# A post-norm transformer block on one core: later batches of x stored whole and split on return, one batch's rows stored after the last maxima

## The chip, the cores and the metric

The kernel runs on one core of a Trainium2 chip. The metric is device time in microseconds of one execution. Engines are TensorE (PE; its weight loads are PEld), VectorE (DVE), ScalarE (ACT), GpSimd (POOL) and SyncE (SP), which here only issues DMAs. ScalarE has a DMA queue of its own as well.

## The reference

The input x has 4 batches of 1024 tokens of 256 features. The block is causal attention with 16 heads of 64 and rotary positions, a layer norm, a mixture of 16 experts of which each token takes 3, and a second layer norm:

```python
x = _layernorm(x + _L0_attn_ref(x, W_in, b_in, W_out, b_out))   # 4 x 1024 x 256, H=16, KD=VD=64
x = _layernorm(x + _L0_ffn_ref(x, gate, W1, b1, W2, b2))        # E=16, top 3, hidden 512
```

All of it is float32. The change touches the attention phase only.

## The kernel before

**Two-part operands.** TensorE's fast format (fp32r) keeps fewer bits than float32. So each operand of the q/k/v projections, x and W_in, is held as a high part (a copy rounded to fp32r, made by ScalarE) and a low part (the operand less its high part, a subtraction on VectorE), and a projection is the sum of high x high, high x low and low x high: `PRODUCTS`, twelve matmuls per projection unit (L583).

**Setup (L270 to L358, L530 to L560, L740 to L760, L845 to L860).** x and the weights are transposed on TensorE (L541) into PSUM banks in units of 512 columns: 12 weight units, 4 units of x per batch, 4 of W_out. For each unit ScalarE writes the high part (`high_halves`, L751) and VectorE the low part (`low_halves`, L856). The weight parts go to the table `wsplit` in DRAM (12 stores of 512 KB, L308). Batch 0 stays in the tile `xT` (index 0 high, 1 low). The units of batches 1 to 3 are transposed after the second projection of pair 0 (`late_transposes`), by ScalarE after the fourth rope copy of pair 0 (`finish_high_halves`), and both their parts are stored in the table `xsplit` (L323, 12 stores of 512 KB); until then they lie in tiles that attention does not need yet (`x_place`). The last two projections of pair 0 come behind them.

**Turns.** Attention takes 32 steps, `n` = batch x 8 + pair of heads. The loop `turns` runs `it` from -2 to 32, and each engine goes through a fixed list per turn: `PE_ORDER`, `ACT_ORDER`, `DVE_ORDER`, `POOL_ORDER`, `SP_ORDER`. A + or - after an event says that it is for a later or earlier step, so `F0++` in turn `it` is of step `it + 2`. The events that matter here:
- F0 to F3: the projections of a step into `g_ps` (F0, F1: q and k for tokens 0 to 511 and 512 to 1023; F2, F3: v). r0 to r3 on VectorE multiply q and k by the rotary tables (L929), a and l on GpSimd add the halves and make the low part (L499, L504), h on ScalarE makes the high part (L803).
- W and S on SP: the high and low parts of q and k go to the table `hilo` (`put_halves`, L336) and come back stacked (`stack`, L350 and L347), in halves c = 0 and 1.
- A: scores by query (L591) whose row maxima VectorE takes (M; L909, L913). One bank per head, so A of one block waits for M of the block before. X transposes the maxima (L700); w on ScalarE (L794) copies them and issues the DMA that puts them as a row beside q (L797).
- B: scores by key less the row of maxima (L598, L599), E: their exponentials on ScalarE (L790). k0 to k3 and K are sums of them on VectorE (L952) and GpSimd (L526), V the product with v (L680), D, R, G and O the normalization and output projection.
- L on SP: loads of the next weights (L406, L410) and, in every eighth turn, the next batch's x from `xsplit` into `xT` (`load_x`, L358, 1 MB for each half of the tokens: half 0 after F0, half 1 after F3 of the batch's last step).
- y and `move_tile`: the first layer norm of a finished batch, spread over the next batch's turns. In the turns 14, 22 and 30 SP stores the rows of batch 0, 1 and 2, two stores of 128 KB per tile, to `xn` and `sum0` (L379, L380).

F0 and F1 of a batch's first step wait for the two halves of x; they are in turns 6, 14 and 22, called borders here. B0 and B4 wait for the rows of maxima of the two halves.

Behind attention come routing, the experts and the final sum with the second layer norm; the change leaves them alone.

Of the kernel before, what the change touches and what calls it, by code (L numbers as in the profile page):

```python
# [17 lines left out]
P = 128  # L18
# [22 lines left out]
ACT_ORDER = parse("""E0.0 E0.1 E1.0 E1.1 E2.0 w1 E2.1 E3.0 d1- h0++ N1- E3.1 E4.0 E4.1 y0 h1++ E5.0 d0 h2++ E5.1 E6.0 N0 E6.1 y1 E7.0  # L41
w0+ E8.0 E7.1 h3++ E8.1 y2 E9.0 E9.1 y3 E10.0 v2++ E10.1 E11.0 E11.1 v3++""")
DVE_ORDER = parse("""M11.1 M0.0+ C0 M0.1+ M1.0+ M1.1+ M2.0+ k0 M2.1+ M3.0+ k1 k2 r0++ M3.1+ R4- r1++ R5- M4.1+ k3 M4.0+ R6- R7-
# [90 lines left out]
def attention_phase(nc, A, dram, shared):  # L134
    x, W_in, b_in, W_out, cosT, sinT = A["x"], A["W_in"], A["b_in"], A["W_out"], A["cos"], A["sin"]
    xsplit, wsplit = dram["xsplit"], dram["wsplit"]
    hilo = dram["hilo"]
    vo = shared["vo"]
    with ExitStack() as ctx:
# [52 lines left out]
        xsp = [sem(f"xsp{b}") for b in range(B)]  # L192
# [40 lines left out]
        for what, p in W_UNITS:  # L233
# [3 lines left out]
        v_flat = v_sb[:, 1].rearrange("p t s c -> p (t s c)").bitcast(F32R)  # L237
        prob_r = prob[:].bitcast(F32R)

        x_place = [[[xT[:, a, k, :] for k in range(DK)] for a in range(2)],  # L240
                   [[q2_flat[1][:, k, :] for k in range(DK)], [v_flat[:, k * T:(k + 1) * T] for k in range(DK)]],
                   [[prob_r[:, (2 * a + k) * T:(2 * a + k + 1) * T] for k in range(DK)] for a in range(2)],
                   [[t[1][:, k, :] for k in range(DK)] for t in (q1, k1)]]

        def setup_places(u):

            if u < NW:
                return w_place[u][:, 0], w_place[u][:, 1]
            b, k, c = X_UNITS[u - NW]
            return [x_place[b][a][k][:, 512 * c:512 * c + 512] for a in range(2)]  # L250
# [20 lines left out]
        def _(sp):  # L271
# [33 lines left out]
            for i, (what, p) in enumerate(W_UNITS):  # L305
                sp.wait_ge(m["setup_hi"], i + 1)
                sp.wait_ge(m["setup_lo"], i + 1)
                sp.dma_start(wsplit[p if what == "qk" else PAIRS + p].rearrange("p (a k c) -> p a k c", a=2, k=DK),  # L308
                             w_place[i].bitcast(F32)).then_inc(m["wsp"], 16)

            sp.wait_ge(m["setup_hi"], EARLY)
# [5 lines left out]
            def put_x(b):  # L317
                sp.wait_ge(m["setup_hi"], NW + 4 * (b + 1))
                sp.wait_ge(m["setup_lo"], NW + 4 * (b + 1))
                dst = xsplit[b].rearrange("p (a k c) -> p a k c", a=2, k=DK)  # L320
                for a in range(2):
                    for k in range(DK):
                        sp.dma_start(dst[:, a, k], x_place[b][a][k].bitcast(F32)).then_inc(xsp[b], 16)  # L323
# [33 lines left out]
            def load_x(batch, c):  # L357
                sp.dma_start(xT[:, :, :, 512 * c:512 * c + 512].bitcast(F32),  # L358
                             row(xsplit, batch).rearrange("p (a k c) -> p a k c", a=2, k=DK)
                             [:, :, :, 512 * c:512 * c + 512]).then_inc(x_ld[c], 16)  # L360
# [11 lines left out]

            def move_tile(b, place, i):
# [3 lines left out]
                if place == LN_STORE and b < B - 1:  # L377
                    sp.wait_ge(m["normed"], TB * b + i + 1)
                    sp.dma_start(xn[b][:, i, :], rows).then_inc(m["x_st"], 16)  # L379
                    sp.dma_start(first_sum[:, TB * b + i, :], rows).then_inc(m["x_st"], 16)  # L380
# [4 lines left out]
            def turn(it, place):  # L385

                for i, (e, ahead) in enumerate(SP_ORDER):
# [8 lines left out]
                    elif kind == "S":  # L396
                        if n == 1 and c == 0:
                            for b in range(1, B):
                                sp.wait_ge(xsp[b], 64)
                        stack(n, s, c // 2, c % 2)  # L400
                    elif c == 0:
                        if more:
                            sp.wait_ge(m["p_fill"], 4 * n + 1)
                            load_x((n + 1) // PAIRS, 0)
                        sp.wait_ge(m["p_fill"], 4 * n + 2)
                        sp.dma_start(flat(w_sb[s]), row(wsplit, (place + ahead + 2) % PAIRS)).then_inc(w_ld[s], 16)  # L406
                    else:
# [4 lines left out]
                        if more:  # L412
                            load_x((n + 1) // PAIRS, 1)
# [1419 lines left out]
```

## Time and profile before

| | us |
|---|---|
| median of 3 runs (1835.59 to 1837.06) | 1836.42 |
| profiled execution, its own time | 1841.24 |
| its span | 1839.4 |
| TensorE busy | 1691.7 (92%) |
| VectorE busy | 1380.8 (75%) |
| GpSimd busy | 1234.6 (67%) |
| ScalarE busy | 729.2 (40%) |
| mean granted clock of TensorE | 0.958 |

The span runs from the first to the last instruction. Matmuls are pipelined, so TensorE's busy share is not its share of peak. The granted clock is a share of 2.4 GHz. "Idle before" in a row is the time for which the engine had no instruction running, with what released it; a letter q behind an engine means its queue, which issues DMAs. Attention ends near 1290 us.

### The profile page before, as it was taken

What the parts mean: (1) busy time and instruction counts of PE and PEld (TensorE: products, weight loads), DVE (VectorE), ACT (ScalarE), POOL (GpSimd) and SP (SyncE); (2) the same over time, 40 slices, a digit from 0 to 9 for tenths busy, and PEclk for the clock granted to TensorE, in tenths of its full rate; (3) what the DMA queues carried; (4) which work ended last, traced back from release to release, by engine and by line L of the source; (5) the groups of instructions that cost most, each with busy time, mean ns of one, the idle gap of its engine ahead of it and who ended that gap; (6) DMA issues with size and microseconds to landing.
All of it is one profiled execution on the core that took longest, in us unless ns stands there. A gap on an engine that the chain in (4) does not pass through costs nothing. (4 is left out here: it accounts for less than half of the span.)

```text
span 1839.4 us, 34097 instructions
## 1 busy us (share of the span) xinstructions
PE 1691.7 (92%) x9515; PEld 1265.7 (69%) x9516; DVE 1380.8 (75%) x3236; ACT 729.2 (40%) x1551; POOL 1234.6 (67%) x1064
## 2 busy tenths in 40 slices
PE   4689999999999999999999999998649999999990
PEld 4566667666766677667766676654339999999980
DVE  3578888888888888888888888865775656656654
ACT  2234444444445544444444444543352222222222
POOL 2256788677877776788777777755017777777764
PEclk8699999999999999999999999989859999999995
DMA  9976556655655776556676664550964444444448
GB/s 308 335 204 163 157 166 202 178 171 151 183 161 173 230 219 190 157 166 198 210 215 187 179 177 138 161 152 1 339 186 70 72 72 75 71 72 74 71 65 277
DMA packets 185572, 302.39 MB, mean 164 GB/s; under 512 B 23632, under 2 KB 82896, under 8 KB 185312
## 3 DMA queue, kind: packets, MB, share of 16 engines
q1 hardware_dynamic: 161872, 269.20, 49.2%
q0 software_dynamic: 21504, 30.29, 10.2%
q10 hardware_dynamic: 2064, 1.31, 0.3%
q8 instruction: 61, 1.00, 0.2%
q14 instruction: 71, 0.58, 0.1%
HBM read 188.81 MB, written 111.67 MB: 163 GB/s over the span
## 5 line engine op out<-in xcount | busy, mean ns | idle before, releaser
L790 ACT ACTIVATE prob<-b_ps 128x512 f32<-128x512 f32 (+3 forms) x768 | 354.5, 488 | 366.7 <-PE b_ps L599 263.8
L526 POOL TENSOR_TENSOR acc<-acc,prob 128x1024 f32<-128x1024 f32 (+1 forms) x192 | 353.0, 1838 | 6.4 <-ACT prob L790 3.3
L598 PE MATMUL b_ps<-q,k 128*128 128x512 f32 (+3 forms) x768 | 296.9, 391 | 7.6 <-ACT prob L790 3.7
L499 POOL TENSOR_TENSOR roped<-rot 128x512 f32<-128x512 f32 x128 | 174.8, 1366 | 166.8 <-DVE rot L929 166.0
L591 PE MATMUL a_ps<-k,q 128*128 128x512 f32 (+3 forms) x768 | 266.7, 384 | 18.2 <-DMA k<-scratch_hilo 8.2
L680 PE MATMUL y_ps<-prob,v_sb 128*64 128x512 f32 (+3 forms) x1536 | 274.9, 493 | 0.1
L909 DVE CUSTOM_DVE_ANT_0 masked<-a_ps,causal 128x128 bf16<-128x128 f32 (+3 forms) x512 | 237.4, 479 | 48.4 <-PE a_ps L591 40.5
L599 PE MATMUL b_ps<-q,k 65*128 65x512 f32 (+3 forms) x768 | 265.0, 349 | 0.0
L1479 POOL DMA_INDIRECT scratch_sum<-y,dst_i x112 | 186.9, 1669 | 94.7 <-ACT y L1551 89.8
L958 DVE RECIPROCAL inv<-inv 128x128 f32<-128x128 f32 x256 | 232.3, 930 | 7.7 <-ACT inv L831 5.3
L504 POOL TENSOR_TENSOR lo<-roped,hi 128x512 fp32r<-128x512 f32 x128 | 177.8, 1389 | 81.1 <-ACT hi L803 81.1
L680 PEld LDWEIGHTS y_ps<-prob,v_sb 128*64 128x64 f32 x1536 | 104.7, 137 | 180.9 <-issue 176.1
L1505 PEld LDWEIGHTS h_ps<-mxT,w_now 128*128 128x128 f32 x1792 | 218.7, 193 | 5.7
L1505 PE MATMUL h_ps<-mxT,w_now 128*128 128x128 f32 x1792 | 219.1, 276 | 0.0
L1514 PE MATMUL yo_ps<-w,hT 128*128 x896 | 211.8, 379 | 0.0
L913 DVE TENSOR_REDUCE max_b<-a_ps 128x1 f32<-128x512 f32 x256 | 171.9, 672 | 41.2 <-PE a_ps L591 37.9
L583 PE MATMUL g_ps<-xT,w_sb 128*128 128x512 f32 x768 | 195.4, 405 | 7.4 <-DVE rot L929 4.5
L598 PEld LDWEIGHTS b_ps<-q,k 128*128 128x128 f32 x768 | 145.3, 189 | 77.2 <-issue 44.9
L591 PEld LDWEIGHTS a_ps<-k,q 128*128 128x128 f32 x768 | 143.2, 192 | 63.3 <-DVE max_b L913 12.3
L1464 POOL DMA_INDIRECT xin<-scratch_xn,src_i x112 | 111.7, 997 | 108.2 <-POOLq L999 74.4
L583 PEld LDWEIGHTS g_ps<-xT,w_sb 128*128 128x128 f32 x768 | 148.7, 197 | 40.3 <-DVE rot L929 5.5
L1514 PEld LDWEIGHTS yo_ps<-w,hT 128*128 128x128 f32 x896 | 161.6, 190 | 17.4
(258 smaller groups left out, 2389.7 us busy)
## 6 DMA issues: line engine op xcount, KB each, us to landing
q<-scratch_hilo SPq DMA_DIRECT2D x192, 256.0 KB, 4.6
k<-scratch_hilo SPq DMA_DIRECT2D x192, 256.0 KB, 5.2
scratch_hilo<-hi SPq DMA_DIRECT2D x64, 512.0 KB, 4.1
scratch_hilo<-lo SPq DMA_DIRECT2D x64, 512.0 KB, 4.7
w_sb<-scratch_wsplit SPq DMA_DIRECT2D x32, 512.0 KB, 3.5
w<-in_L_ffn_W_dram SPq DMA_DIRECT2D x32, 512.0 KB, 10.0
wv_sb<-scratch_wsplit SPq DMA_DIRECT2D x16, 512.0 KB, 7.2
xT<-scratch_xsplit SPq DMA_DIRECT2D x6, 1024.0 KB, 6.6
```

What stands on the lines that cost most here:

```text
L526: nc.gpsimd.tensor_tensor(sums, old, probs(q), ALU.add).then_inc(m["sum_p"], 1)
L583: ins = nc.tensor.matmul(out, left, right, start=(a, b, k) == PRODUCTS[0], stop=(a, b, k) == PRODUCTS[-1], skip_group_check=True)
L591: nc.tensor.matmul(out, q1[s][:, h, blk * P:(blk + 1) * P], k1[s][:, h, k0:k0 + w], start=True, stop=True, skip_group_check=True).then_inc ...
L598: nc.tensor.matmul(out, k1[s][:, h, js], q1[s][:, h, qs], start=True, stop=False, skip_group_check=True)
L599: ins = nc.tensor.matmul(out, k2[s][0:65, h, js], q2[s][0:65, half, h, 512 - w:512], start=False, stop=True, skip_group_check=True)
L680: ins = nc.tensor.matmul(y_ps[64 * h:64 * h + 64, 512 - w:512], v_sb[:, pairs, j, s, 64 * h:64 * h + 64], probs(q)[:, h, :], start=(j == 0 ...
L790: nc.scalar.activation(probs(q)[:, h, :], b_ps[:, h, 0:w], ACT.Exp).then_inc(exp_done[h], 1)
L909: nc.vector.tensor_tensor_reduce(masked[:, h, 0:w], a_ps[:, h, 0:w], causal[:, 512 - w:512], -1.0, -MASKED, ALU.add, ALU.min, out).then_in ...
L958: nc.vector.reciprocal(part, part).then_inc(inv_done[c], 1)
L1479: pool.indirect_dma_start(out=dram[f"sum{t % SUMS}"], out_offset=bass.IndirectOffsetOnAxis(ap=dst_i[:, t:t + 1], axis=0), in_=y[:, t % 2, ...
L1505: ins = nc.tensor.matmul(h_ps[:, s, c * P:(c + 1) * P], w1_now[:, s, k, c * P:(c + 1) * P], xT[:, s, k * P:(k + 1) * P], start=(k == 0), s ...
L1514: ins = nc.tensor.matmul(yo_ps[:, s, 0:D], hT[:, s, c * P:(c + 1) * P], w2[:, bass.ds(e, 1), c, :].rearrange("p a d -> p (a d)"), start=(c ...
```

## The change

What it does, part by part:
- Batches 1 to 3 of x are not split in setup. ScalarE copies each transposed unit as float32 into one whole tile per batch (`x_whole`), and a batch is one store of 1 MB to the table `xturned`, half the bytes of `xsplit`; the 12 subtractions of these batches and TensorE's waits for them are gone.
- On return a half of 512 tokens (512 KB instead of 1 MB) goes to the low place of `xT`. Half 0 is issued by SP as before; half 1 by ScalarE's queue, right behind the last v copy of the batch's last step. New events `s0++` and `s1++` split it: ScalarE copies to the high place (two copies per half), VectorE subtracts in place (two per half). F0 and F1 wait for the subtractions.
- SP stores the six weight units that lie in the way of pair 0's stacks first (`WAITED`), then pair 0's first halves, three other weights, the first stack, the other three weights, the second halves and stack, and then x.
- The rows of batch 2 are stored after the turns, once the last row of maxima has landed (`m_ld`), and no longer in turn 30.

The diff, cut to its core:

```diff
-ACT_ORDER = parse("""E0.0 E0.1 E1.0 E1.1 E2.0 w1 E2.1 E3.0 d1- h0++ N1- E3.1 E4.0 E4.1 y0 h1++ E5.0 d0 h2++ E5.1 E6.0 N0 E6.1 y1 E7.0
+ACT_ORDER = parse("""E0.0 E0.1 s0++ E1.0 E1.1 E2.0 w1 E2.1 s1++ E3.0 d1- h0++ N1- E3.1 E4.0 E4.1 y0 h1++ E5.0 d0 h2++ E5.1 E6.0 N0 E6.1 y1 E7.0
 w0+ E8.0 E7.1 h3++ E8.1 y2 E9.0 E9.1 y3 E10.0 v2++ E10.1 E11.0 E11.1 v3++""")
-DVE_ORDER = parse("""M11.1 M0.0+ C0 M0.1+ M1.0+ M1.1+ M2.0+ k0 M2.1+ M3.0+ k1 k2 r0++ M3.1+ R4- r1++ R5- M4.1+ k3 M4.0+ R6- R7-
+DVE_ORDER = parse("""M11.1 M0.0+ C0 M0.1+ s0++ M1.0+ M1.1+ M2.0+ k0 M2.1+ M3.0+ k1 k2 r0++ M3.1+ s1++ R4- r1++ R5- M4.1+ k3 M4.0+ R6- R7-
 M5.0+ r2++ G1- r3++ z0 M5.1+ o1- M6.0+ R0 M6.1+ R1 M7.0+ R2 R3 G0 z1 M7.1+ o2- M8.0+ M8.1+ M9.0+ o3- M9.1+ M10.0+
...
-        v_flat = v_sb[:, 1].rearrange("p t s c -> p (t s c)").bitcast(F32R)
-        prob_r = prob[:].bitcast(F32R)
-
-        x_place = [[[xT[:, a, k, :] for k in range(DK)] for a in range(2)],
-                   [[q2_flat[1][:, k, :] for k in range(DK)], [v_flat[:, k * T:(k + 1) * T] for k in range(DK)]],
-                   [[prob_r[:, (2 * a + k) * T:(2 * a + k + 1) * T] for k in range(DK)] for a in range(2)],
-                   [[t[1][:, k, :] for k in range(DK)] for t in (q1, k1)]]
+        v_flat = v_sb[:, 1].rearrange("p t s c -> p (t s c)")
+        x_whole = [None] + [t.rearrange("p (k c) -> p k c", k=DK)
+                            for t in (v_flat[:, 0:DK * T], prob[:, 0:DK * T], prob[:, DK * T:2 * DK * T])]
         def setup_places(u):
             if u < NW:
                 return w_place[u][:, 0], w_place[u][:, 1]
             b, k, c = X_UNITS[u - NW]
-            return [x_place[b][a][k][:, 512 * c:512 * c + 512] for a in range(2)]
+            cs = slice(512 * c, 512 * c + 512)
+            return [xT[:, a, k, cs] for a in range(2)] if b == 0 else [x_whole[b][:, k, cs]]
+        WAITED = [u for u in range(NW) if W_UNITS[u][0] == "qk" and 2 <= W_UNITS[u][1]]
+        OTHERS = [u for u in range(NW) if u not in WAITED]
+        def splits_before(n, c):
+            return 4 * (n // PAIRS - 1) + 2 * c
...
+            def put_weights(units, stored):
+                for i in units:
+                    what, p = W_UNITS[i]
+                    sp.wait_ge(m["setup_hi"], i + 1)
+                    sp.wait_ge(m["setup_lo"], i + 1)
+                    sp.dma_start(wsplit[p if what == "qk" else PAIRS + p].rearrange("p (a k c) -> p a k c", a=2, k=DK),
+                                 w_place[i].bitcast(F32)).then_inc(stored, 16)
+            put_weights(WAITED, wsp_first)
...
             def put_x(b):
                 sp.wait_ge(m["setup_hi"], NW + 4 * (b + 1))
-                sp.wait_ge(m["setup_lo"], NW + 4 * (b + 1))
-                dst = xsplit[b].rearrange("p (a k c) -> p a k c", a=2, k=DK)
-                for a in range(2):
-                    for k in range(DK):
-                        sp.dma_start(dst[:, a, k], x_place[b][a][k].bitcast(F32)).then_inc(xsp[b], 16)
+                sp.dma_start(xturned[b].rearrange("p (k c) -> p k c", k=DK), x_whole[b]).then_inc(xsp[b], 16)
...
-            def load_x(batch, c):
-                sp.dma_start(xT[:, :, :, 512 * c:512 * c + 512].bitcast(F32),
-                             row(xsplit, batch).rearrange("p (a k c) -> p a k c", a=2, k=DK)
-                             [:, :, :, 512 * c:512 * c + 512]).then_inc(x_ld[c], 16)
+            def load_x(batch):
+                sp.dma_start(xT[:, 1, :, 0:512].bitcast(F32),
+                             row(xturned, batch).rearrange("p (k c) -> p k c", k=DK)[:, :, 0:512]).then_inc(x_ld[0], 16)
...
+            def put_tile(b, i):
+                rows = x1[:, b % 2 * TB + i, :]
+                sp.wait_ge(m["normed"], TB * b + i + 1)
+                sp.dma_start(xn[b][:, i, :], rows).then_inc(m["x_st"], 16)
+                sp.dma_start(first_sum[:, TB * b + i, :], rows).then_inc(m["x_st"], 16)
             def move_tile(b, place, i):
                 rows = x1[:, b % 2 * TB + i, :]
-                if place == LN_STORE and b < B - 1:
-                    sp.wait_ge(m["normed"], TB * b + i + 1)
-                    sp.dma_start(xn[b][:, i, :], rows).then_inc(m["x_st"], 16)
-                    sp.dma_start(first_sum[:, TB * b + i, :], rows).then_inc(m["x_st"], 16)
+                if place == LN_STORE and b < B - 2:
+                    put_tile(b, i)
...
-                        if n == 1 and c == 0:
-                            for b in range(1, B):
-                                sp.wait_ge(xsp[b], 64)
...
-            for c in range(2):
-                put_halves(0, 0, c)
-            sp.wait_ge(m["wsp"], 16 * NW)
-            for c in range(2):
-                for second in range(2):
-                    stack(0, 0, c, second)
-                put_x(1 + c)
-            put_x(3)
+            put_halves(0, 0, 0)
+            put_weights(OTHERS[:3], m["wsp"])
+            sp.wait_ge(wsp_first, 16 * len(WAITED))
+            for second in range(2):
+                stack(0, 0, 0, second)
+            put_weights(OTHERS[3:], m["wsp"])
+            put_halves(0, 0, 1)
+            for second in range(2):
+                stack(0, 0, 1, second)
+            for b in (2, 3, 1):
+                put_x(b)
+            sp.wait_ge(m["wsp"], 16 * len(OTHERS))
             for it in range(-2, STEPS):
                 turn(it, it)
+            for c in range(2):
+                sp.wait_ge(m_ld[c], 16 * STEPS)
+            for i in range(TB):
+                put_tile(B - 2, i)
...
-                    pe.wait_ge(m["setup_lo"], old + 1)
+                    if u < EARLY:
+                        pe.wait_ge(m["setup_lo"], old + 1)
...
-                        if q < 2 and not first:
-                            pe.wait_ge(x_ld[q], 16 * (n // PAIRS + 1))
+                        if q < 2 and n >= PAIRS:
+                            pe.wait_ge(m["setup_lo"], EARLY + splits_before(n, q) + 2)
...
+                    elif kind == "s":
+                        if n % PAIRS or n == 0:
+                            continue
+                        act.wait_ge(x_ld[q], 16 * (n // PAIRS + 1))
+                        for k in range(DK):
+                            nc.scalar.activation(xT[:, 0, k, 512 * q:512 * q + 512],
+                                                 xT[:, 1, k, 512 * q:512 * q + 512].bitcast(F32),
+                                                 ACT.Copy).then_inc(m["setup_hi"], 1)
...
+                        if q == 3 and n % PAIRS == PAIRS - 1 and n + 1 < STEPS:
+                            act.dma_start(xT[:, 1, :, 512:T].bitcast(F32),
+                                          xturned[(n + 1) // PAIRS].rearrange("p (k c) -> p k c", k=DK)[:, :, 512:T])\
+                                .then_inc(x_ld[1], 16)
...
+                    elif kind == "s":
+                        if n % PAIRS or n == 0:
+                            continue
+                        for k in range(DK):
+                            dve.wait_ge(m["setup_hi"], NW + NX + splits_before(n, q) + k + 1)
+                            low = xT[:, 1, k, 512 * q:512 * q + 512]
+                            nc.vector.tensor_tensor(low, low.bitcast(F32), xT[:, 0, k, 512 * q:512 * q + 512].bitcast(F32),
+                                                    ALU.subtract).then_inc(m["setup_lo"], 1)
...
-                        if n == 0 and q == 3:
-                            low_halves(EARLY, NW + NX)
```

Three places show what moved. SP's queue in the opening, before, from the last rows of the weight stores: `wsplit` is the weights' table, `hilo` the table of q and k, whose halves come back into the q and k tiles, `xsplit` the table of split x.

```order
L308 DMA scratch_wsplit<-q_1 128x1024 x2
L308 DMA scratch_wsplit<-k_1 128x1024
L336 DMA scratch_hilo<-hi 256x1x512
L336 DMA scratch_hilo<-lo 256x1x512
L336 DMA scratch_hilo<-hi 256x1x512
L336 DMA scratch_hilo<-lo 256x1x512
L350 DMA q_0<-scratch_hilo 64x2x512 x2
L350 DMA k_0<-scratch_hilo 64x2x512 x2
L347 DMA q_0<-scratch_hilo 64x2x512
L347 DMA k_0<-scratch_hilo 64x2x512
L323 DMA scratch_xsplit<-q_1 128x1024 x2
```

And of the change, from the first weight stores:

```order
L316 DMA scratch_wsplit<-q_0 128x1024 x2
L316 DMA scratch_wsplit<-k_0 128x1024 x2
L316 DMA scratch_wsplit<-q_0 128x1024 x2
L341 DMA scratch_hilo<-hi 256x1x512
L341 DMA scratch_hilo<-lo 256x1x512
L316 DMA scratch_wsplit<-w_sb 128x1024 x2
L316 DMA scratch_wsplit<-wv_sb 128x1024
L355 DMA q_0<-scratch_hilo 64x2x512 x2
L355 DMA k_0<-scratch_hilo 64x2x512 x2
L352 DMA q_0<-scratch_hilo 64x2x512
L352 DMA k_0<-scratch_hilo 64x2x512
L316 DMA scratch_wsplit<-q_1 128x1024 x2
```

Six weight stores, not twelve, stand before the first hi and lo of pair 0; the second hi and lo moved behind the first stack and three more weight stores; x has three stores, and they come after the second stack.

VectorE at the start of turn 6, before, from the maxima of the first block of scores (128x128) to those of the second (128x256):

```order
L909 ISA masked,max_a<-a_ps,causal 128x128
L909 ISA max_a 128x1
L920 TENSOR_TENSOR max_c<-max_b 128x8
L909 ISA masked,max_a<-a_ps,causal 128x128
L909 ISA max_a 128x1
L909 ISA masked,max_a<-a_ps,causal 128x256
L909 ISA max_a 128x1
L909 ISA masked,max_a<-a_ps,causal 128x256
```

And of the change:

```order
L931 ISA masked,max_a<-a_ps,causal 128x128
L931 ISA max_a 128x1
L950 TENSOR_TENSOR max_c<-max_b 128x8
L931 ISA masked,max_a<-a_ps,causal 128x128
L931 ISA max_a 128x1
L945 TENSOR_TENSOR xT<-xT 128x512 x2
L931 ISA masked,max_a<-a_ps,causal 128x256
L931 ISA max_a 128x1
```

The two subtractions of x's first half stand before the maxima of the second block (128x256). The other two stand behind the fourth block's second maxima, before the second rope:

```order
L959 SCALAR_TENSOR_TENSOR rot<-g_ps,bias,cos_sb 128x512
L959 SCALAR_TENSOR_TENSOR rot<-g_ps,bias,sin_sb 128x512
L931 ISA masked,max_a<-a_ps,causal 128x512
L931 ISA max_a 128x1
L945 TENSOR_TENSOR xT<-xT 128x512 x2
L986 RECIPROCAL inv<-inv 128x128
L959 SCALAR_TENSOR_TENSOR rot<-g_ps,bias,cos_sb 128x512
L959 SCALAR_TENSOR_TENSOR rot<-g_ps,bias,sin_sb 128x512
L986 RECIPROCAL inv<-inv 128x128
```

ScalarE's copies for them stand behind the first two exponentials of the turn and behind the sixth.

## Rows read from the trace of the kernel before

**Rows 1.** Windows: length, busy us (PE, PEld, DVE, ACT, POOL), clock, DMA share, GB/s
```profile
34.00:40.00 6.00, 4.98 (x13) 3.87 (x14) 0.96 (x2) 0.74 (x2) 3.83 (x3) 0.54 1.03 418
...
110.00:116.00 6.00, 5.67 (x18) 4.55 (x19) 2.27 (x5) 1.21 (x2) 3.60 (x4) 0.72 0.39 80
...
200.00:300.00 100.00, 100.00 (x535) 71.26 (x535) 86.36 (x187) 45.13 (x97) 77.46 (x68) 1.00 0.61 171
```

**Rows 2.** The query by line, transposes of the first maxima: duration, first and last start
```profile
L700 PE MATMUL t_ps<-ident,max_a x32: 271/273/274, 81.8 to 1234.8; 128*8 128x128 f32 x32
```

**Rows 3.** TensorE's waits: total us, times, longest
```profile
PE a_ps L591 <- DMA k<-scratch_hilo: 8.2, 4, 3.5
```

**Rows 4.** The timeline, opening: start, us, engine, line; copies and transposes
```profile
46.96 1.07 ACT L751 ACTIVATE q<-b_ps 128x512 fp32r<-128x512 f32 x2
...
48.41 1.09 PE L541 MATMUL b_ps<-ident,yT 128*128 128x128 f32 x4 [6.57 <-DVE v_sb L856]
...
56.28 1.19 ACT L757 ACTIVATE woT<-a_ps 128x512 f32<-128x512 f32 x2
```

**Rows 5.** The timeline, opening: a load of the table, TensorE after it
```profile
54.71 1.28 SPq L350 DMA_DIRECT2D q<-scratch_hilo  x2
...
62.62 0.44 PE L591 MATMUL a_ps<-k,q 128*128 128x128 f32 x2 [1.95 <-DMA k<-scratch_hilo]
...
74.80 1.22 PE L591 MATMUL a_ps<-k,q 128*128 128x512 f32 x2 [3.48 <-DMA k<-scratch_hilo]
...
75.88 5.12 PE L583 MATMUL g_ps<-xT,w_sb 128*128 128x512 f32 x12
```

**Rows 6.** The timeline, turn 0: VectorE's rope and TensorE
```profile
109.40 0.74 DVE L929 SCALAR_TENSOR_TENSOR rot<-g_ps,bias,sin_sb 128x512 f32<-128x512 f32 x1
...
110.33 0.73 PE L591 MATMUL a_ps<-k,q 128*128 128x512 f32 x2 [2.35 <-DMA k<-scratch_hilo]
...
111.53 4.34 PE L583 MATMUL g_ps<-xT,w_sb 128*128 128x512 f32 x12
```

**Rows 7.** The timeline, start of turn 6: exponentials, maxima, TensorE
```profile
320.70 1.79 ACT L790 ACTIVATE prob<-b_ps 128x512 f32<-128x512 f32 x3
...
321.63 0.42 DVE L909 CUSTOM_DVE_ANT_0 masked<-a_ps,causal 128x256 bf16<-128x256 f32 x1
...
322.11 0.19 PEld L591 LDWEIGHTS a_ps<-k,q 128*128 128x128 f32 x1 [0.16 <-DVE max_a L909]
```

**Rows 8.** The timeline, turn 6: GpSimd's add, the second rope, its projection
```profile
328.28 1.27 POOL L499 TENSOR_TENSOR roped<-rot 128x512 f32<-128x512 f32 x1 [2.48 <-DVE rot L929]
...
330.33 0.74 DVE L929 SCALAR_TENSOR_TENSOR rot<-g_ps,bias,sin_sb 128x512 f32<-128x512 f32 x1
...
332.33 2.90 PE L583 MATMUL g_ps<-xT,w_sb 128*128 128x512 f32 x12
```

**Rows 9.** The timeline, VectorE with two inputs: setup, turn 6, turn 31
```profile
16.50 0.69 DVE L856 TENSOR_TENSOR q<-a_ps,q 128x512 fp32r<-128x512 f32 x1 [0.16 <-ACT q L751]
...
332.67 0.88 DVE L952 TENSOR_TENSOR acc<-acc,prob 128x256 f32<-128x256 f32 x1
...
1257.24 0.42 DVE L952 TENSOR_TENSOR acc<-acc,prob 128x256 f32<-128x256 f32 x1 [0.83 <-ACT prob L790]
```

**Rows 10.** The timeline, turns 30 and 31: row of maxima, TensorE
```profile
1214.28 0.63 ACTq L797 DMA_DIRECT2D q<-mrow  x1
...
1220.99 0.77 PE L598 MATMUL b_ps<-q,k 128*128 128x512 f32 x1 [2.47 <-DMA q<-mrow]
...
1231.55 0.50 PE L598 MATMUL b_ps<-q,k 128*128 128x512 f32 x1
...
1255.87 0.45 PE L598 MATMUL b_ps<-q,k 128*128 128x512 f32 x1
...
1261.07 0.50 PE L598 MATMUL b_ps<-q,k 128*128 128x512 f32 x1
```

**Rows 11.** The windows, turn 30
```profile
1221.00:1224.00 3.00, 2.89 (x6) 1.78 (x6) 0.92 (x2) 0.67 (x2) 0.00 (x0) 0.50 0.81 274
```

More of the change, by code:

```diff
@@ L135, in attention_phase @@
     x, W_in, b_in, W_out, cosT, sinT = A["x"], A["W_in"], A["b_in"], A["W_out"], A["cos"], A["sin"]
-    xsplit, wsplit = dram["xsplit"], dram["wsplit"]
+    xturned, wsplit = dram["xturned"], dram["wsplit"]
     hilo = dram["hilo"]
@@ L191, in attention_phase @@
         m = {k: sem(k) for k in names}
-        xsp = [sem(f"xsp{b}") for b in range(B)]
+        wsp_first = sem("wsp_first")
+        xsp = [None] + [sem(f"xsp{b}") for b in range(1, B)]
         x_in = [sem(f"x_in{b}") for b in range(B)]
@@ L303, in _ @@
             sp.dma_start(wo_raw, W_out.rearrange("(r p) c -> p r c", p=P)).then_inc(m["wo_in"], 16)
[L305 to L309, printed above, removed]
+            def put_weights(units, stored):
[6 more added lines that the diff above has]
+            put_weights(WAITED, wsp_first)
             sp.wait_ge(m["setup_hi"], EARLY)
@@ L403, in turn @@
                             sp.wait_ge(m["p_fill"], 4 * n + 1)
-                            load_x((n + 1) // PAIRS, 0)
+                            load_x((n + 1) // PAIRS)
                         sp.wait_ge(m["p_fill"], 4 * n + 2)
@@ L411, in turn @@
                                 .then_inc(m["wv_ld"], 16)
-                        if more:
-                            load_x((n + 1) // PAIRS, 1)
                 if ZEROS_FROM <= it < ZEROS_FROM + ZERO_PIECES:
@@ L554, in late_transposes @@
                     transposes(NW + NX + i, [wo_raw[:, r, (4 * c + j) * P:(4 * c + j + 1) * P] for j in range(4)])
-                pe.wait_ge(m["setup_lo"], NW + NX)
                 pe.wait_ge(m["wo_ev"], len(WO_UNITS))
@@ L744, in high_halves @@
                     act.wait_ge(m["setup_tr"], u + 1)
-                    if u >= NW and X_UNITS[u - NW] == (3, 0, 0):
-                        act.wait_ge(m["wsp"], 16 * NW)
                     src = setup_bank(u)
@@ L772, in turn @@
                             for b in range(1, B):
-                                act.wait_ge(xsp[b], 64)
+                                act.wait_ge(xsp[b], 16)
                         act.wait_ge(b_fill[h], UNITS * n + q + 1)
@@ L1789, in scratch @@
 def scratch(nc):
-    shapes = {"xsplit": [B, P, 2 * DK * T], "wsplit": [PAIRS + PAIRS // 2, P, 2 * DK * 256], "hilo": [2, 2, P, 2, T], "xn": [NTOK, E_ + D]}
+    shapes = {"xturned": [B, P, DK * T], "wsplit": [PAIRS + PAIRS // 2, P, 2 * DK * 256], "hilo": [2, 2, P, 2, T], "xn": [NTOK, E_ + D]}
     shapes.update({f"sum{i}": [NTOK + P, D] for i in range(SUMS)})
```

## The prediction

> **What bounds the kernel now.** I read the windows first. In the middle of attention TensorE is busy for all 100 us of 100, at a granted clock of 1.00, its 2.4 GHz [rows 1]; a turn lasts 37.2 us on average, 31 of them from 81.8 to 1234.8 us [rows 2]. So in a turn nothing is gained by taking work off another engine, and each us for which TensorE is made to wait is a us of the end. The list of its waits and the timeline say where it does wait: 6.57 us once for a low half of x, at 48.41; 8.2 us in four waits for k from the hi/lo table [rows 3], the three large ones at 62.62, 74.80 and 110.33; and 2.47 us for the row of maxima at 1220.99, in turn 30 [rows 4, 5, 6, 10]. The change can win only there. It can lose wherever a new wait enters a full turn.
>
> **The opening.** Batches 1 to 3 are no longer split: 12 subtractions leave VectorE, and 3 MB of 6 leave the stores. The copies of those units begin at 46.96; ScalarE is held until then by the rope of pair 0, so the wait of 6.57 us hardly shrinks. The last of 16 copies ends at 57.47, after steps partly in turn with VectorE. ScalarE alone does two in 1.07 us, so twelve in 6.4, and the four of W_out at 0.60 in 2.4: the end comes at 55.8, 1.6 us sooner [rows 4]. The last two projections of pair 0 then end at 59.1 instead of 60.7 (62.62 less 1.95), where the first score waits for k [rows 5]. That load was issued at 54.71, behind twelve weight stores and the first hi/lo halves. A store of 512 KB takes 1.25 us at the 418 GB/s of a full queue [rows 1]. Six fewer stand ahead now, so it is issued at about 47.2. From issue to use it took 7.9 us; with the three weight stores that stand before it added (3.8) it is there at 58.9, and the wait goes. Scores start 3.5 us sooner.
>
> The second half of pair 0 gains less. Its path is 47.2, three stores (3.8), six loads (1.5 MB; 7.5 us if a load of 256 KB takes as long as a store, half that at the full rate), three stores and two halves (6.3), and 7.9 from issue to use: 72.7 or 68.9, against 74.80 now, so 2.1 us, or at most 3.5, since the rope would then set the projection that follows at 75.88. I take 2.4, between them and nearer to the slow one, as loads of 2 KB rows are; 1.0 is kept as the low end. Pair 1's first half then comes in time (0.4, the smallest of the four waits). The 2.35 us at 110.33 go as well, since 3 MB of stores, 7.5 us, no longer lie in the queue; but the projection behind them needs VectorE's rope, which ends at 110.14, so it moves only from 111.53 to 110.2: 1.3 us. It ran in 4.34 us, where twelve such matmuls take 2.90 at full clock [rows 6, 8], because the clock fell behind that idle stretch: 0.72 over these 6 us [rows 1]. With 1.1 us idle instead of 2.35 I expect it full: 1.4 us more (bounds 0 and 1.4). Opening: 2.4 + 0.4 + 1.3 + 1.4 = **5.5 us gained** (2.7 to 6.6).
>
> **Turn 30.** The row of maxima is issued at 1214.28; TensorE is ready at 1218.5 and waits until 1220.99 [rows 10]; then the clock reads 0.50, 1.2 GHz [rows 11]. Sixteen stores of batch 2's rows share the DMA engines there. They now go out after the last row of maxima, under work of turn 31. What stays ahead is 1 MB of loads, 2.5 us at the full rate, which would end before 1218.5 and leave no wait; the other end is no gain at all. I take 1.6 of the 2.47, nearer to the first. With 0.9 us idle the clock should hold. From this matmul to the one at 1231.55 it is 10.56 us; in turn 31 the same work but for three score matmuls takes 5.20 (1255.87 to 1261.07), and those three with a wait for VectorE make some 2.1: 3.3 us saved. Together **4.9 us** (bounds 0 and 5.8). The stores' new place costs nothing: SP's queue holds nothing else then, and 16 stores of 128 KB are 5 us at the full rate, under a turn.
>
> **The borders, turns 6, 14 and 22.** Each gains four copies on ScalarE and four subtractions on VectorE. Start of the turn: ScalarE's second exponential ends near 321.9 (three in 1.79 us from 320.70). Then come a copy of 128x512 (0.60, an exponential's) and a subtraction (0.69, the setup's, [rows 9]); the second copy is hidden, the second subtraction is not. The next maxima began at 321.63; now at 321.9 + 0.6 + 0.69 + 0.69 = 323.9. TensorE already waits 0.16 us for just these [rows 7], and its stream is in order, so it stands still for **2.25 us** in front of the first projection. Behind that projection the other two subtractions stand before the second rope. This rope ends at 331.07, the projection that needs it starts at 332.33: 1.26 us of slack [rows 8]. Two subtractions are 1.4 us by the plain price. But a VectorE operation with two inputs in SBUF took 0.88 us while GpSimd was adding, and the same shape 0.42 while it was not [rows 9], and an add of GpSimd of 1.27 us falls on this place [rows 8]. So I take 2.1, and 0.9 is left over on TensorE. The Trainium skill has the rule (SBUF — State Buffer, "SBUF: two separate sides"): VectorE with two SBUF inputs and GpSimd shut each other out for a whole instruction. The trace agrees with it; without the rule the leftover would be 0.1. A border costs 3.2 us (2.3 to 4.4, if the backlog also delays the third rope). The issue on ScalarE's queue runs beside a copy of 0.60 us and is taken as free (0.6 at most). Of the smaller loads I count nothing: no wait is theirs today.
>
> On top comes the clock. It fell after 2.35 us of idle time in turn 0 and after 2.47 in turn 30, so a border's 2.25 is on the edge. A fall costs 4.34 - 2.90 = 1.4 us; I count it at one or two borders of three, 2.1 us. Borders: 3 x 3.2 + 2.1 = **11.7 us lost** (7 to 17).
>
> **Sum.** -5.5 - 4.9 + 11.7 = +1.3 us. The profiled execution took 1841.24 us (span 1839.4), 4.8 above the median of the runs shown, 1836.42; applied to the median: **1837.7 us**. Routing, experts and the final sum do not move.
>
> **The rivals.** First, *the splits hide*. For it: VectorE idles 14 us in 100 [rows 1]. Against it: the start of the turn is its densest place. If a border costs 1.5 us and the gains stand, -10.4 + 4.5 = -6: 1830.5. Second, *the clock falls at every border* and VectorE's backlog reaches the third rope: 3 x (4.4 + 1.4) = 17.4, less 10.4: +7, 1843.4. This is the case on the other side; it decides from about 2.3 us of idle time at a border, and a copy 0.1 us slower than I take it is enough. The Trainium skill (TensorE: Matmul & The Clock Gate, "HAM oscillation — how this bites in real kernels") warns of idle gaps that put TensorE back to half its clock; the rows of turns 0 and 30 agree. Third, *the stores were not the cause*: the row of maxima lands late behind the 1 MB of loads alone, and x's second half, on ScalarE's queue but the same engines, holds ScalarE: +1.3 + 4.9 = +6, 1842.6. By the Trainium skill (DMA: Bandwidth & Descriptors, "Issuing engines are not separate DMA queues") a second queue saves only the issue; no run here shows that. That the change does not do what it says has no room: the printed order shows each moved row.
>
> **How the numbers follow.** The sum as worked out, 0.42; splits hide, 0.27; clock at every border, 0.18; stores not the cause, 0.13. A measurement of this kernel tells 0.2%, 3.7 us, from no change. So faster 0.27, same 0.42, slower 0.31. The likeliest case alone has 1834 to 1840. The range goes from 1829.5 (opening and end at their upper bounds, -12.4, borders at 1.8 each, +5.4) to 1845 (the second rival with 4 us of opening: 17.4 - 8.9 = +8.5).
>
> **What would show it.** Right: the waits at 62.62 and 1220.99 gone or under 1 us, clock 1.00 through turn 30, and in turns 6, 14 and 22 a wait of some 2 us of TensorE for the maxima behind the first split. Wrong: border turns that last no longer than before, or a clock of 0.50 in each of them, or the row of maxima still awaited for over 2 us in turn 30.

## The result and the profile after

The changed kernel takes 1843.82 us (median of 19 runs) and the kernel before 1837.11 us (19 runs): a ratio of 1.0034, with a 95% interval of 1.0026 to 1.0042. So it is slower by 0.34%, 6.3 us, above the 1837.7 us forecast and inside the range of 1829.5 to 1845.0. The prediction drew its own line between same and slower at 3.7 us; by that line this is slower. The profiled execution took 1846.57 us (span 1844.4).

TensorE's waits in the list by line, in the columns of [rows 3]:

```profile
PE a_ps L604 <- DVE max_a L931: 6.7, 6, 2.0
PE g_ps L596 <- DVE rot L959: 6.5, 4, 4.5
...
PE a_ps L604 <- DMA k<-scratch_hilo: 5.5, 1, 5.5
PE b_ps L611 <- DMA q<-mrow: 5.4, 3, 2.8
```

Four waits for k (8.2 us) have become one of 5.5. New are three waits of 2 us for the maxima (first line), three of 0.67 for the rope (in the second, beside an old one of 4.5), and three for a row of maxima, where the kernel before had 2.7 us in two. To see what this does to a turn, take the transposes of the first maxima, [rows 2], in pairs: first and last start of two neighbours are one turn apart. After, for turns 0, 6, 14, 22 and 30:

```profile
L713 PE MATMUL t_ps<-ident,max_a x2: 272/272/273, 78.0 to 119.8; 128*8 128x128 f32 x2
L713 PE MATMUL t_ps<-ident,max_a x2: 273/273/273, 302.5 to 343.6; 128*8 128x128 f32 x2
L713 PE MATMUL t_ps<-ident,max_a x2: 272/272/273, 604.2 to 644.4; 128*8 128x128 f32 x2
L713 PE MATMUL t_ps<-ident,max_a x2: 272/272/273, 903.5 to 945.3; 128*8 128x128 f32 x2
L713 PE MATMUL t_ps<-ident,max_a x2: 273/274/274, 1205.8 to 1239.5; 128*8 128x128 f32 x2
```

And before, turns 0 and 30:

```profile
L700 PE MATMUL t_ps<-ident,max_a x2: 271/272/274, 81.8 to 122.2; 128*8 128x128 f32 x2
L700 PE MATMUL t_ps<-ident,max_a x2: 273/274/274, 1194.7 to 1234.8; 128*8 128x128 f32 x2
```

The opening gave 3.8 us up to the first transpose, of which turn 0 took 1.4 back. The borders last 41.2, 40.2 and 41.7 us instead of 37.0, 37.4 and 37.5: 11.2 us lost. Turn 30 fell from 40.1 to 33.7: 6.4 gained. From the last transpose to the end both need 604.7 to 604.9 us. The other turns add some 2.4 us, which closes the account to the 5.0 us between the spans; nearly all of it are waits of 1.21 and 1.32 us for a row of maxima in turns 10 and 23.

A border in the timeline, turn 6, beside [rows 7, 8]:

```profile
319.19 1.14 ACT L814 ACTIVATE xT<-xT 128x512 fp32r<-128x512 f32 x2
...
319.85 1.29 DVE L945 TENSOR_TENSOR xT<-xT 128x512 fp32r<-128x512 f32 x2 [0.74 <-ACT xT L814]
321.06 0.41 DVE L931 CUSTOM_DVE_ANT_0 masked<-a_ps,causal 128x256 bf16<-128x256 f32 x1
...
321.54 0.44 PE L604 MATMUL a_ps<-k,q 128*128 128x384 f32 x1 [1.99 <-DVE max_a L931]
...
323.65 4.03 PE L596 MATMUL g_ps<-xT,w_sb 128*128 128x512 f32 x12
327.16 1.15 ACT L814 ACTIVATE xT<-xT 128x512 fp32r<-128x512 f32 x2 [2.76 <-DMA xT<-scratch_xturned]
...
329.21 1.27 POOL L512 TENSOR_TENSOR roped<-rot 128x512 f32<-128x512 f32 x1 [3.90 <-DVE rot L959]
...
329.65 1.99 DVE L945 TENSOR_TENSOR xT<-xT 128x512 fp32r<-128x512 f32 x2
...
333.78 0.50 PE L596 MATMUL g_ps<-xT,w_sb 128*128 128x512 f32 x1 [0.67 <-DVE rot L959]
```

VectorE sits idle for 0.74 us until the copy is there, subtracts for 1.29, and only then takes the maxima for which TensorE has been waiting 1.99 us. The projection behind it takes 4.03 us instead of 2.90, for the clock has fallen. Two subtractions of the second half take 1.99 us beside GpSimd's add, and 0.67 is left over for TensorE. The windows of turns 6, 22, 14 and 30, in the columns of [rows 1]:

```profile
323.00:325.00 2.00, 2.00 (x7) 1.68 (x7) 1.99 (x5) 0.65 (x3) 0.85 (x2) 0.50 1.08 255
924.00:926.00 2.00, 2.00 (x9) 1.81 (x8) 1.17 (x6) 1.02 (x3) 0.41 (x1) 0.50 1.02 369
625.00:627.00 2.00, 2.00 (x11) 1.67 (x11) 1.89 (x6) 1.27 (x5) 0.58 (x2) 1.00 1.02 363
1213.00:1223.00 10.00, 10.00 (x62) 8.52 (x60) 7.74 (x19) 4.93 (x12) 9.83 (x9) 1.00 0.85 246
```

The clock is 0.50 behind the wait of turns 6 and 22 and 1.00 behind that of turn 14, and it stays at 1.00 through turn 30.

In turn 0 the wait for k at 110.33 [rows 6] is gone, and one for the row of maxima is there (run 2 will show that the old opening can have that one too). The timeline, TensorE in the opening, then ScalarE's queue and TensorE in turn 0:

```profile
71.09 1.22 PE L604 MATMUL a_ps<-k,q 128*128 128x512 f32 x2 [5.46 <-DMA k<-scratch_hilo]
...
100.48 0.63 ACTq L807 DMA_DIRECT2D q<-mrow  x1
...
107.61 0.77 PE L611 MATMUL b_ps<-q,k 128*128 128x512 f32 x1 [2.83 <-DMA q<-mrow]
```

The wait in turn 10 has no store of rows near it. SP's load of 512 KB ahead of it, the row's own DMA, and TensorE:

```profile
468.73 0.33 SPq L417 DMA_DIRECT2D wv_sb<-scratch_wsplit  x1
...
472.62 0.63 ACTq L807 DMA_DIRECT2D q<-mrow  x1
...
480.68 0.47 PE L611 MATMUL b_ps<-q,k 128*128 128x512 f32 x1 [1.21 <-DMA q<-mrow]
```

Between the load of wv_sb and the row stand two loads of 256 KB from the table. Nothing else is issued in the 3.8 us ahead of the row, and yet TensorE gets it only 8.1 us after its issue.

### The profile page after: what moved, and what is told of

Same layout as the page of the kernel before. It is cut to its first block and busy times, and to the rows that moved or that the text cites. A ratio compares the mean times of both kernels' runs of the same rounds, so it can differ in the third digit from the quotient of the medians.

```text
span 1844.4 us, 34087 instructions
## 1 busy us (share of the span) xinstructions
PE 1692.1 (92%) x9515; PEld 1269.9 (69%) x9516; DVE 1379.5 (75%) x3236; ACT 733.9 (40%) x1563; POOL 1234.5 (67%) x1064
## 5 line engine op out<-in xcount | busy, mean ns | idle before, releaser
L525 POOL TENSOR_SCALAR_AFFINE_SELECT prob<-prob 128x256 f32<-128x256 f32 x256 | 110.3, 436 | 95.7 <-ACT prob L800 90.8
```

## The experiments

Theory T after this comparison: the splits cost some 3.7 us a border, and where they stand is the cause; the stores of turn 30 held up the row of maxima; the opening gains, and a new wait in turn 0 limits it. Ratios are to the kernel before, on the same chip; 1 us is 0.00054. Beside the time, the length of single turns is compared, since a run's profile is one execution.

**1. Batch 2's rows in turn 30 again** (the changed kernel otherwise).

```diff
-                if place == LN_STORE and b < B - 2:
+                if place == LN_STORE and b < B - 1:
...
-            for i in range(TB):
-                put_tile(B - 2, i)
```

> The changed kernel, but batch 2's rows are stored in turn 30 again, as before. Theory T (the stores held up the row of maxima; the border turns and not the end cost time): turn 30 lasts some 6.4 us longer than in the changed kernel (40.1 instead of 33.7 us from one transpose of maxima to the next), TensorE waits 2 to 2.5 us for the row of maxima and the clock falls to 0.50 behind it; the whole is 6 us slower than the changed kernel, some 12 us (0.7%) slower than the kernel before. Rival R1 (turn 30's gain comes from the smaller loads of x or from another alignment, not from the stores): turn 30 stays near 34 us and the time within 2 us of the changed kernel.

Measured: 1.0045 (1.003 to 1.0059). Turn 30 lasts 37.6 us, and TensorE waits 0.89 us for the row where the kernel before showed 2.47:

```profile
1226.06 0.47 PE L607 MATMUL b_ps<-q,k 128*128 128x512 f32 x1 [0.89 <-DMA q<-mrow]
```

Against the changed kernel's 1.0034 the stores cost 2 us, with both intervals taken together anything from none to 5 us, and not the 6 of theory T. The two traces with the stores in this place show that the row is late by a different amount in each execution.

**2. The kernel before, with the rows stored last.**

> The kernel before with one part of the change: batch 2's rows are stored after the last row of maxima. Theory T: turn 30 goes from 40.1 to some 33.7 us, all other turns stay, and the whole is 5 to 6.4 us faster than the kernel before (ratio 0.997). Rival R1: turn 30 keeps a wait of 2 us, since the 1 MB of loads alone delay the row of maxima, and the time stays within 1.5 us. Rival R4 (the stores behind the turns delay the start of routing): turn 30 gains and the phase behind it gives 2 us or more back.

Measured: 0.9986 (0.9971 to 1.0), 2.6 us faster (0 to 5.3). Turn 30 lasts 33.7 us and holds no wait for the row, as T had it, but the time gains less than half of 6.4. Routing's first transpose comes 1.0 us later behind the last turn; its last one comes 0.7 us earlier, so of R4 nothing is left in this trace.

Its turn 0, whose opening is that of the kernel before, shows something else. The wait for k at 110.33 isn't there, and TensorE waits for the row of maxima instead:

```profile
111.73 0.77 PE L605 MATMUL b_ps<-q,k 128*128 128x512 f32 x1 [2.87 <-DMA q<-mrow]
```

So neither wait belongs to one kernel. Which of the two comes in turn 0 differs from execution to execution, with the old opening too.

**3. The first half split one turn earlier**, in gaps of VectorE; the second half as before. In this and the next kernels s0 to s3 are VectorE's four subtractions, ScalarE's s0 and s1 the copies of a half.

```diff
-ACT:  E0.0 E0.1 s0++ E1.0        ...  h3++ E8.1
+ACT:  E0.0 E0.1 E1.0             ...  h3++ s0+++ E8.1
-DVE:  M0.1+ s0++ M1.0+   M3.1+ s1++ R4-        M7.1+ o2- M8.0+ M8.1+
+DVE:  M0.1+ M1.0+        M3.1+ s2++ s3++ R4-   M7.1+ s0+++ o2- M8.0+ s1+++ M8.1+
```

> The changed kernel, but the first half of x is copied and subtracted one turn earlier (its load has landed some 10 us before that turn ends), each subtraction in a gap of VectorE. Theory T (a border costs 2.0 us for the first split, 1.2 us for the clock behind it and 0.7 us for the second split): the wait of 2.0 us in front of the border's first projection and the fall of the clock go, turns 6, 14 and 22 last 37.5 to 38.5 us instead of 41.2, 40.2 and 41.7, and the whole is 8 to 10 us faster than the changed kernel, 2 to 4 us faster than the kernel before. Rival R2 (the load of the second half on ScalarE's queue and its split are what costs): the borders keep more than 2 us each. Rival R3 (VectorE is short in that turn anyway, so the work only moves): the turns before the borders grow by 1 us or more each and the gain is under 6 us.

Measured: 0.9977 (0.9963 to 0.9991), 4.2 us faster than the kernel before and some 10.5 faster than the changed one. The waits of 2 us and the falls of the clock are gone; the borders last 38.3 us each, the turns before them 36.7, 37.3 and 37.3 as ever. Theory T holds, R2 and R3 fall. What is left is a wait of 0.59 to 0.68 us for the second rope. The load has landed long before: it is issued at 282.92 and lands at 287.08, and the subtractions run at 304.38 and 306.68. The second of them in the timeline, with GpSimd's add beside it:

```profile
304.85 2.85 POOL L539 TENSOR_TENSOR acc<-acc,prob 128x1024 f32<-128x1024 f32 x1
...
306.68 1.58 DVE L945 TENSOR_TENSOR xT<-xT 128x512 fp32r<-128x512 f32 x1
```

**4. The kernel before with the rows last and the opening's stores sorted** as in the change; x split in setup. (In code: the order of the stores as in the diff ahead, with the weights in q1 and k1 ahead of the other three.)

> The kernel before with batch 2's rows stored last (as in the run beside it) and the weight stores of the opening sorted as in the change, while x is still split in setup and stored as 6 MB. Theory T: most of the opening's gain (scores start sooner) comes from the order of the stores, so this is 1 to 3 us faster than the run with the rows alone, some 8 us faster than the kernel before, and faster than any kernel with splits in the borders as they stand. Rival R5 (the gain comes from the 3 MB fewer): it is within 1 us of the run with the rows alone, or slower, since the later stores collide with the loads of turn 0.

Measured: 1.0005 (0.9991 to 1.0019). Not faster than run 2, rather 3.5 us slower. The first transpose comes at 78.4 (before 81.8), so the order does gain 3.4 us; but 3 MB more stand in the queue, and turn 0 then lasts 44.1 us:

```profile
100.91 0.48 PE L608 MATMUL a_ps<-k,q 128*128 128x128 f32 x1 [5.24 <-DMA k<-scratch_hilo]
```

This is what R5 had: without the halved bytes the order gives back in turn 0 what it gained ahead of it. The intervals of runs 2 and 4 overlap, so the times alone don't prove that it is slower than run 2; that the order alone does not bring the 1 to 3 us of theory T is fairly sure.

**5. The changed kernel again**, beside runs 6 to 8.

> The changed kernel itself, unaltered, beside the three variants on one chip, so that they can be compared with it directly. Theory T: the three borders last 3 to 5.5 us more than the kernel before's each, in any execution; turn 0 has a wait for a row of maxima of 1 to 3 us; whole: ratio 1.0034 as in the first comparison, bounds 1.002 and 1.005.

Measured: 1.0037 (1.0022 to 1.0052). Borders of 41.3, 41.7 and 41.7 us; waits of 2.00, 1.87 and 1.87 us with the clock at 0.50 behind all three; the row of maxima of turn 0 awaited for 1.29 us.

**6. As 3, and in border turns a reciprocal behind the second rope.**

```diff
-DVE, turns 6, 14, 22:  s2++ s3++ R4- r1++
+DVE, turns 6, 14, 22:  s2++ s3++ r1++ R4-
```

> The kernel with the first half split early, and in the three border turns a reciprocal (R4) moved behind the second rope of VectorE, so that the two subtractions of the second half stand where the reciprocal stood. Theory T (what is left at a border is VectorE's backlog of 0.6 us in front of the second projection): this wait goes, and each border gives 0.6 to 1.0 us, 2 to 3 us in all against the kernel with the early split (its ratio was 0.9977), so 0.996 to 0.997. Rival R6 (the backlog only moves on to the third rope or to the output projection that waits for the reciprocal): the borders stay at 38.3 us and the time within 1 us.

Measured: 0.9986 (0.997 to 1.0001). The waits for the second rope are gone and the borders last 38.0 us, 0.3 less than in run 3, which is half of what I expected at the least. In the time nothing shows: run to run its times lie between 1831.3 and 1844.0 us. Neither side was right: the waits went, as T had it, and the time stayed, as R6 had it.

**7. As 6, with turn 0's loads held** until the second row of maxima has landed.

```diff
+                        if it == 0:
+                            sp.wait_ge(m_ld[1], 16)
                         sp.wait_ge(m["p_fill"], 4 * n + 4)
```

> As the run before, and in turn 0 alone SP issues the load of wv_sb (512 KB) and the next two loads of the table hilo only when the second row of maxima has landed. Theory M (these loads stand in front of the 4 KB row of maxima on the DMA engines, and so TensorE waits 0.9 to 2.9 us for it near 105 us): the wait goes, turn 0 lasts 38 us instead of 40 to 42, the whole is 2 to 3 us faster than without. Rival M2 (the row needs its 6 to 7 us whatever is in flight): the wait stays above 1 us and nothing is gained; or the held loads come late and turn 1 waits for k.

Measured: 0.9979 (0.9966 to 0.9992), 1.3 us faster than run 6; the intervals overlap. Turn 0 lasts 38.8 us, and a wait of 0.52 us for the row is left. This proves nothing for M: run 6's own trace has no wait for the row in turn 0 (it lasts 39.9 us there), and the time can't tell the two runs apart.

**8. The loads held in every turn** (`if it >= 0: sp.wait_ge(m_ld[1], 16 * n)` in the same place), and **9. the same kernel once more**, beside runs 10 to 12.

> As the run with turn 0's loads held, but in every turn the load of wv_sb and the two loads behind it wait until the second row of maxima has landed. Theory M: the scattered waits of 0.5 to 1.3 us for rows of maxima in turns 10, 23 and 30 go as well; 0 to 2 us faster than with turn 0 alone. Rival M3 (the held loads are needed at once in later turns, where SP's list is tight): waits for k or for the stack appear in many turns, and the time is 2 us or more worse.

> The fastest kernel so far (first half split early, reciprocal behind the rope, loads held in all turns), unaltered, as the measure for the three beside it: ratio 0.996, its times within some 5 us of each other.

Measured: 0.9959 (0.9948 to 0.9971) and 0.9967 (0.9958 to 0.9976), 7.5 and 6.1 us faster than the kernel before. Run 8 is 3.7 us faster than run 7, with intervals that overlap a little, and some 5 us faster than run 6. In the turns behind turn 0 no wait over 0.1 us for a row of maxima is left, and none for k, so M3 falls. All five traces with the loads held in every turn (runs 8 to 12) are free of waits for the row there, where six of the nine others have one or two of 0.4 to 2.5 us. In turn 0 a wait of 0.54 and 0.30 us stays. The times of twelve executions each lie within 5.4 and 6.2 us, where those of runs 6 and 7 lay within 12.7 and 10.5. So the held loads took some of the spread away; that it was this wait is likely and not shown. This version beats both kernels.

**10. The kernel before with rows last and loads held.**

> The kernel before with two parts: batch 2's rows last, and the loads held in all turns until the second row of maxima has landed; x is split in setup and stored as 6 MB as before. Theory W (x whole is worth it once its splits are early: the opening gains 5 to 6 us at the first transpose of turn 1, the borders lose 2.5 to 3.5): 2 to 4 us slower than the run beside it, ratio near 0.998, with waits for k at 62, 75 and 110 us as in the kernel before. Rival W2 (the hold and the place of the rows made all of the gain): the same as the run beside it or faster.

Measured: 1.0067 (1.005 to 1.0083), 12.3 us slower than before and 18 slower than run 9. W had the sign, not the size, and the reason is one that I had not seen: in the kernel before, SP issues x's second half (1 MB) behind the load that is held now. It goes out at 325.46 instead of 321.06, and at 922.74 in turn 22:

```profile
922.74 0.59 SPq L358 DMA_DIRECT2D xT<-scratch_xsplit  x1
...
933.77 2.47 PE L592 MATMUL g_ps<-xT,w_sb 128*128 128x512 f32 x5 [4.87 <-DMA xT<-scratch_xsplit]
```

So this run doesn't price the whole x by itself. It shows that the hold costs more than it brings while x's half stands behind the held load in SP's list. Whether the other queue or the halved bytes is what spares the changed kernel this, no run separates. Its turn 0 has no wait for k either, against what W had expected at 110 us.

**11. As 9, with the rows in turn 30.**

> The run beside it with batch 2's rows stored in turn 30 again. The two traces with this placing showed waits for the row of maxima of 2.47 and 0.89 us. Theory S (the stores delay it by a different amount in each execution, 0.9 to 2.5 us, and the clock falls only behind the long ones): 2 to 4 us slower on the average, and the times spread wider. As the prediction had it: 4.9 us slower. Rival S2 (with the loads held nothing else stands in front of the row): within 1 us.

Measured: 0.9966 (0.9955 to 0.9977), the same as run 9, as S2 had it. SP's last issue ahead of the row, the row's DMA, and SP's first issues once it has landed:

```profile
1204.96 0.43 SPq L387 DMA_DIRECT2D scratch_sum<-x1b  x1
...
1208.57 0.63 ACTq L809 DMA_DIRECT2D q<-mrow  x1
...
1210.34 0.32 SPq L423 DMA_DIRECT2D wv_sb<-scratch_wsplit  x1
1210.71 0.43 SPq L386 DMA_DIRECT2D scratch_xn<-x1b  x1
```

The hold keeps back more than the load: the stores of seven of the eight tiles stand behind it in SP's list, and they go out at 1210.71 and later. So the run shows that these stores cost nothing when they follow the row. It doesn't show that they were harmless where they stood. Here the row is there at most 1.8 us after its issue. In the kernel before it was issued at 1214.28 and awaited until 1220.99 [rows 10], 6.7 us. In the 3 us ahead of it SP had issued the load of wv_sb, two loads of the table and three stores there, and more stores followed; in run 11 SP had issued nothing for 3.6 us. Which share is the loads' and which the stores', these runs don't separate. Turn 10 of the change has such a wait with loads alone ahead of it.

**12. As 9, with the second halves ahead of the last three weight stores.**

```diff
-            put_weights(OTHERS[3:], m["wsp"])
             put_halves(0, 0, 1)
             for second in range(2):
                 stack(0, 0, 1, second)
+            put_weights(OTHERS[3:], m["wsp"])
```

> The run beside it, but SP issues the last three weight stores of the opening behind pair 0's second halves and their stack instead of ahead of them. TensorE waits 4.7 to 6.9 us for k at 70 to 71 us there. Theory Q (three stores of 512 KB stand in front: 3.8 us at the full rate): this wait shrinks by 3 to 4 us and the whole by as much, ratio 0.994. Rival Q2 (the path is the halves' own: the rope copies they wait for end late, so they cannot be issued sooner, and the table's way out and back takes some 17 us): under 1.5 us. Rival Q3 (the stores then collide with turn 0's loads, and the row of maxima or k is late there): gained at 70, given back near 90 to 110.

Measured: 0.9959 (0.9944 to 0.9974), not told apart from run 9.

```profile
66.49 1.05 PE L610 MATMUL a_ps<-k,q 128*128 128x512 f32 x2 [1.39 <-DMA k<-scratch_hilo]
...
69.24 2.31 PE L602 MATMUL g_ps<-xT,w_sb 128*128 128x512 f32 x5 [1.70 <-DVE rot L965]
...
103.48 1.12 PE L610 MATMUL a_ps<-k,q 128*128 128x512 f32 x2 [1.69 <-DMA k<-scratch_hilo]
```

The wait for k shrinks from 6.9 to 1.4 us, as Q had it, but the rope is late next (1.7), and a wait for k appears in turn 0 (1.7): the first transpose comes 2.3 us sooner than in run 9, the second 1.4. That is Q with Q3's return; the time can't tell it.

## Why the prediction was right in its range and wrong in its number

**The opening: forecast 5.5, found 6.1, by other steps.** That the totals are close is luck. Over the five traces with the changed opening as it stands (the change, runs 1, 3, 5, 6) the first transpose comes at 76.8 us on average and the second at 116.9; over the two with the old one (before, run 2) at 81.9 and 123.1. Ahead of turn 0 the gain is thus 5.1, where I had 2.4. The wait at 62.62 went as said, but I took the second half at 72.7, "nearer to the slow one", and it is used at 70.0 to 71.1, in the middle of my two ends. That is 4.1 us sooner on average, more than the "at most 3.5": I had kept the rope where it was, and it ends at 69.7 instead of 75.8. Most of the last us is the clock's: the projection behind it took 5.12 us before and 3.8 to 5.1 after. In turn 0 the gain is 1.1 instead of 3.1 (0.4 + 1.3 + 1.4). The step that failed is "The 2.35 us at 110.33 go as well": that was one execution. Of the three traces with the old opening (before, runs 2 and 10) only the first has this wait, and run 2 has 2.87 us for the row of maxima in its place. With the new opening TensorE waits 0.9 to 2.8 us for the row in four of the five traces, with a fall of the clock behind all but the shortest wait.

**Borders: forecast 11.7, found 12.2.** The three traces with these borders (the change, runs 1 and 5) give 11.2, 12.5 and 12.8 us over the kernel before. The mechanism was right in each part: the first split keeps TensorE waiting for 1.86 to 2.00 us (I had 2.25), the second for 0.67 (I had 0.9), a border without a fall of the clock costs 2.7 (I had 3.2). The failed step is "I count it at one or two borders of three": it fell at 7 of the 9 borders, for some 1.5 us each and once for twice as long, which is 4.0 us an execution instead of 2.1. The smaller price of the splits hid most of that in the sum, and this is luck as well. Run 5 shows the clock at 0.50 at all three borders, which the prediction had named as a sign that it is wrong. Run 3 shows that the place of the first split was the cause: with it one turn earlier the same four copies and four subtractions cost 1 us a border.

The Trainium skill (SBUF — State Buffer, "SBUF: two separate sides") says that a VectorE operation with two inputs in SBUF, as these subtractions are, and a GpSimd operation that reads SBUF exclude each other for the whole instruction. The rows of run 3 agree: the subtraction begins at 306.68, GpSimd's add ends at 307.70, and the subtraction ends 0.56 us after it, near its own 0.69. In turns 13 and 21 the same subtraction again ends 0.55 and 0.56 us after the add.

**Turn 30: forecast 4.9, found 2 to 2.6 in the time**, though the profile shows 6.4. The weak step is the first: "TensorE is ready at 1218.5 and waits until 1220.99" is one execution. Run 1 has the stores and waits 0.89 us. Runs 1 and 2 put the average at 2 and 2.6 us, but their intervals reach from nothing to 5 us, so that 4.9 was too much is likely and not certain. The cause was also drawn too narrowly: waits of 1.21 and 1.32 us for the row stand in turns 10 and 23 of the change, and in turn 10 only loads stand ahead of it. Run 11 shows no wait once the load and seven tiles' stores go out behind the row.

**The sum.** With the terms as found, -6.1 + 12.2 - 2.3 = +3.8 us; measured are +6.3 (4.8 to 7.7). The range held; the likeliest case, 1834 to 1840 us, did not, and what came is the slower case with its 0.31. Both mistakes, the clock at the borders and the end, lay on the side of the slow outcome. The waits for rows of maxima in other turns (2.5 us in one trace of the change, 0.6 and none in the two others, 1.0 on average) bring it to 4.8; the rest, 1 to 2 us, stays open, as does why these waits are there at all in the change. The time that came true lies next to the second rival's (+7), "the clock falls at every border", but not by its sum: the clock fell at 7 of 9, and the backlog at the third rope did not show. Of the third rival, that the end gains nothing, about half was true by the averages of runs 1 and 2.

## What to carry to other kernels

A term that is read as one wait of a DMA in one execution is a sample: give it a range down to what the same row would be without the collision, and weigh it by the average. When a transfer is taken out of a queue, list every small transfer that shares the stretch, for the next wait can be among them. Conversion work that a load needs before use belongs where its engine has a gap, a turn before its use if the data can be there; and a small, urgent DMA can be helped by holding back the large loads that nobody needs yet, provided nothing urgent is queued behind them.

## What was not expected of the hardware

- A row of 4 KB took at most 1.8 us from issue to landing when SP had issued nothing for 3.6 us (run 11), some 6.7 in turn 30 of the kernel before and 8.1 in turn 10 of the change, although it is issued on ScalarE's queue and the loads are on SP's. The Trainium skill (DMA: Bandwidth & Descriptors, "Issuing engines are not separate DMA queues") says that DMAs of all queues interleave on the same 16 engines; these numbers agree.
- Equal waits do not give equal clocks. Behind nine waits of 1.86 to 2.00 us at borders the granted clock fell to 0.50 seven times. Behind a wait of 1.24 to 1.26 us in turn 30, which twelve traces show with nothing longer than 0.5 us just ahead of it, it fell three times to 0.50, which is 1.2 GHz, and such a turn lasts 35.2 us where the others last 33.6 to 34.3.
